# Sixteen square tiles for s, full-height products for n, and one path for all sixteen batches, in a linear attention chain

## The reference, cut to what matters

```
for i in range(12):                      # attention without a softmax, so every step is linear
    q, k, v = split(x @ Wqkv[i].T + bqkv[i])      # 16 heads of 8 channels
    att = einsum('bhqd,bhkd->bhqk', q, k) * scale
    y = einsum('bhqk,bhkd->bhqd', att, v)
    x = y @ Wproj[i].T + bproj[i] + x
x = layernorm(x0 + x)
x = layernorm(x + ffn(x))                # silu(gate) * up, hidden size 384
```

## Time and profile before

| | us |
|---|---|
| median of 3 runs | 310.84 (309.97 to 310.84) |
| span of the profiled execution | 308.2 |
| outside the span, against the median | 2.6 |
| PE busy | 302.1 (98%) |
| DVE, ACT, POOL busy | 216.9, 192.0, 133.8 |
| one layer, from an H stage to the next (L1097 at 101.95 and 121.95) | 20.00 |

### The profile page before, as it was taken

How to read it: one execution, slowest core, us unless ns; L and a number is a source line. 1 busy time by engine, 2 the same in 40 slices (tenths; PEclk the granted TensorE clock), 3 DMA queues, 4 the chain that set the end, 5 groups by cost and what they waited for, 6 DMA issues and landing times.

```text
span 308.2 us, 9599 instructions
## 1 busy us (share of the span) xinstructions
PE 302.1 (98%) x4010; PEld 283.8 (92%) x4010; DVE 216.9 (70%) x651; ACT 192.0 (62%) x459; POOL 133.8 (43%) x142
## 2 busy tenths in 40 slices
PE   8999999999999999999999999999999999999994
PEld 8989999899998998989989999899998889999983
DVE  0477586676876768758677587676765997888874
ACT  3458667686585675865758668577586276444451
POOL 3064180480723806418045072360634663655533
PEclk9999999999999999999999999999999999999999
DMA  7603003030030210300203002020000000121112
GB/s 265 265 2 113 6 6 109 4 113 2 2 115 3 74 43 4 113 4 10 105 5 113 2 3 79 4 75 6 5 0 2 2 2 0 37 64 41 34 35 72
DMA packets 8908, 14.96 MB, mean 49 GB/s; under 512 B 800, under 2 KB 5280, under 8 KB 8864
## 3 DMA queue, kind: packets, MB, share of 16 engines
q1 hardware_dynamic: 8144, 13.34, 13.1%
q10 hardware_dynamic: 720, 0.99, 0.9%
HBM read 12.23 MB, written 2.10 MB: 46 GB/s over the span
## 4 chain that ended last, share of the span: by engine, by line
PE 96%; DMA 1%; DVE 1%; POOLq 0%; issue 0%; POOL 0%; ACT 0%; SPq 0%
PE ps L988 14%; PE ps L1097 14%; PE ps L1063 13%; PE ps L1218 7%; PE ps L946 6%; PE ps L945 6%; PE ps L944 6%; PE ps L1027 4%; PE ps L1007 4%; PE ps L1206 4%; PE ps L1207 4%; PE ps L1178 2%; PE ps L1038 2%; PE ps L961 2%; PE ps L1014 2%; PE ps L999 2%
## 5 line engine op out<-in xcount | busy, mean ns | idle before, releaser
L428 POOL TENSOR_TENSOR wq_lo<-w,wq_hi 128x512 fp32r<-128x512 f32 x12 | 15.3, 1279 | 112.7 <-ACT wq_hi L551 112.7
L466 POOL TENSOR_TENSOR step_lo<-step,step_hi 128x512 fp32r<-128x512 f32 (+1 forms) x44 | 48.9, 1144 | 13.4 <-ACT step_hi L574 13.4
L944 PE MATMUL ps<-state_hi,step_hi 128*128 128x258 f32 x154 | 44.4, 288 | 0.0
L946 PE MATMUL ps<-state_hi,step_lo 128*128 128x258 f32 x154 | 43.6, 283 | 0.0
L945 PE MATMUL ps<-state_lo,step_hi 128*128 128x258 f32 x154 | 43.5, 282 | 0.0
L988 PE MATMUL ps<-w,gram 128*128 128x128 f32 x352 | 42.8, 275 | 0.0
L988 PEld LDWEIGHTS ps<-w,gram 128*128 128x128 f32 x352 | 41.9, 192 | 0.6
L547 ACT COPY gk<-ps 128x512 f32<-128x512 f32 x48 | 28.1, 586 | 21.3 <-PE ps L988 21.3
L1097 PE MATMUL ps<-step,gram 128*128 128x128 f32 x320 | 40.6, 281 | 0.0
L574 ACT CAST step_hi<-step 128x512 fp32r<-128x512 f32 (+1 forms) x44 | 24.7, 566 | 24.7 <-DVE step L764 24.7
L1097 PEld LDWEIGHTS ps<-step,gram 128*128 128x128 f32 x320 | 37.3, 192 | 1.3
(11 more groups left out here) (148 smaller groups left out, 671.2 us busy)
## 6 DMA issues: line engine op xcount, KB each, us to landing
w<-weights SPq DMA_DIRECT2D x12, 592.5 KB, 3.8
xchan<-x_chan SPq DMA_DIRECT2D x8, 256.0 KB, 4.0
out<-xchan SPq DMA_DIRECT2D x7, 256.0 KB, 2.3
xt<-x_tok SPq DMA_DIRECT2D x4, 258.0 KB, 5.5
xt<-x_tok ACTq DMA_DIRECT2D x3, 258.0 KB, 5.3
fw_int<-ffn_weights SPq DMA_DIRECT2D x1, 576.0 KB, 5.0
cst<-consts SPq DMA_DIRECT2D x1, 147.5 KB, 6.9
xt<-x_tok SPq DMA_DIRECT2D x1, 129.0 KB, 2.6
```

What stands on the lines that cost most here:

```text
L466: nc.gpsimd.tensor_tensor(step_part(step_lo, g, True), step_part(step, g, True), step_part(step_hi_f, g, True), ALU.subtract).then_inc(ste ...
L944: nc.tensor.matmul(dst, l_hi, r_hi, start=True, stop=False)
L946: return nc.tensor.matmul(dst, l_lo, r_hi, start=False, stop=True)
```

## The change

1. **S on square tiles.** A product now takes 32 rows and 32 columns: one batch, one quad. There are 64 in place of 16, in rounds of four with all four row strips and all four column strips. In round k strip i of the rows goes to strip (i + k) mod 4 of the PSUM partitions, in bank k, so that after four rounds all sixteen tiles of the array have been used once. Bank k then holds the quads of a pair of batches turned by k strips: all 128 rows of it are the s of one pair. The first half of S waits once for two blocks of `mt` (before: for one, and after its first four products for the second).
2. **N over 128 rows.** `lay_out` stores in place of the four repeated quads four copies of wq, the kth with its rows turned by k quads, so a pair's s is multiplied in one product of 128 rows that sums the four quads. Three float32 products and one of three passes for batches 0 to 7, four of three passes for batches 8 to 15: 18 products in place of 72.
3. **Waits by pair of banks.** ACT copies `s_rows` in two pieces of 256 columns, and N's first products wait for a piece each; `n_done` counts four times a layer and DVE adds the identity per group of four batches. `step`'s groups are now four neighbouring batches, and H runs group by group.
4. **No batches apart.** `b_whole`, `state_whole`, the stage at L1038 and the products at L1121 are gone. Batches 14 and 15 go through the three passes of U, and their splits, copies and low parts are made as for all the others. `mu_ready` of the last pair now comes after the copy of B's high part.

The diff, cut:

```diff
-                nc.scalar.copy(s_rows[:, 0:2, :], s_banks(0)[:, 0:2, :]).then_inc(s_low_half_ready, 1)
+                for i in range(2):
+                    nc.scalar.copy(s_rows[:, i, :], s_banks(0)[:, i, :]).then_inc(s_low_half_ready, 1)
                 act.wait_ge(s_done, at(2, 2))
...
+                for i in range(0, QUADS, 2):
+                    nc.scalar.copy(s_hi[:, i:i + 2, :], s_banks(1)[:, i:i + 2, :]).then_inc(s_hi_ready, 1)
...
-                    if g % 2 == 0:
-                        dve.wait_ge(n_done, at(2, g // 2 + 1))
+                    dve.wait_ge(n_done, at(GROUPS, g + 1))
...
-                if not first:
-                    for b in range(WHOLE):
-                        dve.wait_ge(b_whole_done, at(WHOLE, b + 1) - WHOLE)
-                        nc.vector.tensor_copy(b_whole[:, b, :], b_whole_out(b)).then_inc(b_whole_ready, 1)
...
-                    if e < SPLIT_PAIRS:
-                        dve.wait_ge(b_hi_ready, at(SPLIT_PAIRS, e + 1))
-                    else:
-                        dve.wait_ge(gram_ready, at(PAIRS, PAIRS))
                     place = 2 * (e % 2)
...
+                    dve.wait_ge(b_hi_ready, at(PAIRS, e + 1))
...
 # S
-                        pe.wait_ge(m_ready, at(GROUPS, GROUPS if h else j + 1))
-                        for i in range(QUADS):
-                            r = slice(QUAD * i, QUAD * (i + 1))
-                            place = GB * (2 * h + j)
-                            last = nc.tensor.matmul(s_banks(h)[:, i, P * j:P * (j + 1)],
-                                                    mt[r, place:place + QUADS, :].rearrange("p b i -> p (b i)"),
...
+                    pe.wait_ge(m_ready, at(GROUPS, GROUPS if h else 2))
                     for j in range(2):
+                        for k in range(QUADS):
+                            b = 2 * (QUADS * h + k) + j
+                            for i in range(QUADS):
+                                own, r = slice(QUAD * i, QUAD * (i + 1)), QUAD * ((i + k) % QUADS)
+                                last = nc.tensor.matmul(ps[r:r + QUAD, HALF_BANKS[h].start + k, P * j:P * (j + 1)], mt[own, b, :],
+                                                        wp_cent[own, :] if last_layer else w[own, s, WP:WP + P],
+                                                        start=True, stop=True)
...
 # N
+                    for k in range(QUADS):
+                        turned = slice(P * k, P * (k + 1))
+                        out_k = n_bank(h, k)
+                        if h == 0 and k < QUADS - 1:
+                            if k < 2:
+                                pe.wait_ge(s_low_half_ready, at(2, k + 1))
+                            else:
+                                pe.wait_ge(s_high_half_ready, at(1, 1))
+                            last = nc.tensor.matmul(out_k, w[:, s, WQ + P * k:WQ + P * (k + 1)], s_rows[:, k, :], start=True, stop=True)
+                        elif h == 0:
+                            pe.wait_ge(s_quad_hi_ready, at(1, 1))
+                            nc.tensor.matmul(out_k, wq_hi[:, turned], s_quad_hi[:, :], start=True, stop=False)
+                            pe.wait_ge(wq_lo_ready, at(1, 1))
+                            nc.tensor.matmul(out_k, wq_lo[:, turned], s_quad_hi[:, :], start=False, stop=False)
+                            pe.wait_ge(s_quad_lo_ready, at(1, 1))
+                            last = nc.tensor.matmul(out_k, wq_hi[:, turned], s_quad_lo[:, :], start=False, stop=True)
                         else:
+                            if k % 2 == 0:
+                                pe.wait_ge(s_lo_ready, at(2, k // 2 + 1))
+                            last = three_pass(out_k, wq_hi[:, turned], wq_lo[:, turned], s_hi[:, k, :], s_lo[:, k, :])
+                        if k % 2 == 1:
+                            last.then_inc(n_done, 1)
...
-                if not first:
-                    b_whole_stage()
...
-                        if b >= SPLIT:
-                            last = nc.tensor.matmul(ps[:, two.start + k, 0:P + 2], step[:, b, :], state_whole[:, b - SPLIT, :],
-                                                    start=True, stop=True)
-                            continue
...
-        wts[:, :, WQ + P * r:WQ + P * (r + 1)] = np.tile(wqkv[:, QUAD * r:QUAD * (r + 1)], (1, QUADS, 1))
+        wts[:, :, WQ + P * r:WQ + P * (r + 1)] = np.roll(wqkv[:, 0:P], QUAD * r, axis=1)
```

More of the change, by code:

```diff
@@ L360, in n_banks, with n_bank @@
             return ps[:, HALF_BANKS[h], 2 * P:4 * P]
+        def n_bank(h, k):
+            return ps[:, HALF_BANKS[h].start + k, 2 * P:4 * P]
         def pair_banks(e):
@@ L465, in layer @@
                     pool.wait_ge(step_hi_ready, at(GROUPS, g + 1))
-                    nc.gpsimd.tensor_tensor(step_part(step_lo, g, True), step_part(step, g, True), step_part(step_hi_f, g, True),
+                    nc.gpsimd.tensor_tensor(group(step_lo, g), group(step, g), group(step_hi_f, g),
                                             ALU.subtract).then_inc(step_lo_ready, 1)
@@ L1088, in layer @@
                     return
-                for q in range(GROUPS):
-                    if q == 2:
+                for g in range(GROUPS):
+                    if g == 2:
                         shift_stage(s, at(1, 1))
-                    pe.wait_ge(step_ready, at(GROUPS, q + 1))
-                    for g in (q // 2 * 2, q // 2 * 2 + 1):
-                        for b in range(GB * g + 2 * (q % 2), GB * g + 2 * (q % 2) + 2):
-                            last = nc.tensor.matmul(one_product(H_BANKS[g], b), gram_raw[:, b, 0:P] if first else gram[:, b, :],
-                                                    step[:, b, :], start=True, stop=True)
-                        if q % 2 == 1:
-                            last.then_inc(h_done, 1)
-                pe.wait_ge(mu_split, at(2, 2))
+                    pe.wait_ge(step_ready, at(GROUPS, g + 1))
+                    for b in range(GB * g, GB * (g + 1)):
+                        last = nc.tensor.matmul(one_product(H_BANKS[g], b), gram_raw[:, b, 0:P] if first else gram[:, b, :],
+                                                step[:, b, :], start=True, stop=True)
+                    last.then_inc(h_done, 1)
+                pe.wait_ge(mu_split, at(1, 1))
                 for e in range(PAIRS):
@@ L1133, in a_stage @@
                 for b in range(GB * g, GB * (g + 1)):
-                    left = b_whole[:, b - SPLIT, :] if b >= SPLIT else bsum[:, b, :]
-                    last = nc.tensor.matmul(one_product(A_BANKS[g], b), left, step[:, b, :], start=True, stop=True)
+                    last = nc.tensor.matmul(one_product(A_BANKS[g], b), bsum[:, b, :], step[:, b, :], start=True, stop=True)
                 last.then_inc(a_done, 1)
```

102 lines of the change are left out of this document (20 added, 82 removed).

## The result

The changed kernel takes 321.25 us (median of 4 runs, 320.8 to 322.1) against 310.46 us (309.97 to 310.84) for the kernel before on the same chip: 1.035 times the time, 95% interval 1.033 to 1.038, or 10.8 us more. The prediction was 306.5 us, and the sign is wrong. The profiled execution has a span of 319.9 us against 308.2, so 11.7 us have to be found. (The two differences are not the same, since the profiled runs are not the medians. In every run the time lies 1.8 to 1.9 us above its own span, so the profiled runs are those of 309.97 and 321.71.)

What follows compares the result with a forecast made beforehand. PE, busy 98% of the span, was taken as the bound. Middle layers at -0.40 us gave -4.0 for ten, layer 0 -0.26, the last -0.05: sum -4.3, span 303.9, time 306.5 us; eight-in-ten range 305.1 to 308.6.

Steps and rivals of the forecast that it cites:

- S's price: S: 64 square products at about 0.014 us each take 0.88 where S took 0.93 before, so nothing is lost.
- Rival 1: S: fewer than sixteen tiles run at once, so slower; 314.5 us at eight, 334 at four, about 465 singly; chance 7%.
- When S begins: Start of S: waiting for two blocks of mt moves it from 136.89 to 136.92, +0.03 us.
- ACT's copy decides N's start: Between S and N: ACT's 256-column copy ends at 138.09 and releases N at 138.15; S would allow 138.02.
- Gain 0.51 per layer: Between S and N: without B's two products, N starts at 138.15 in place of 138.66.
- N and H: N's length stays; H follows 0.12 us behind N in place of 0.23, with a usual first record: gain 0.21.
- forecast wait of 0.05 for the quad's low part: In N: the fourth quad's low part comes from POOL late, so its pass runs at 139.84 in place of 139.79.
- U: In U: two float32 products of 0.45 us together go and six passes of 0.12 come: loss 0.27 per layer.
- cover of 0.13: At U's end: the last pair's means take 1.10 us, the load is wanted at 1.23, so no cost.
- no cost: Layers: POOL gets 0.5 us more, DVE and ACT some 0.8, within their idle time, so the time does not change.
- Rows that share a bank: S: four row strips write one bank at once; allowed by the bank-and-quadrant unit, else strips go one after another.

Runs made afterwards that it cites:

- line 999 four times: The kernel before with its own square stage (16 products of kdiag times rows) issued four times in a row, result unchanged: 336.98 us.
- a quarter of the columns: The changed kernel with each of S's products on 32 of 128 columns, all instructions kept and the rest of s left out: 318.24 us.
- both streams shifted: The kernel before with part 4 of the change only, plus 24 one-column memsets on DVE and 16 one-column products on PE at the start: 319.44 us, ratio 1.028.
- part 4 alone: The kernel before without the batches apart, S and N otherwise as before: 314.56 us, ratio 1.014.

## Why the prediction was wrong, point by point

- **S's price: wrong, and this is the step that failed.** "The starts are thus spread over 0.22, about 0.014 per product ... all 64 take 0.88." The product count is paid for by the width in the first 32 records only. 64 products take 1.64, 0.0256 each. The forecast named the limit at which it would be wrong (records more than 0.011 apart); they are 0.0128 apart. I took shape, size and type as what makes a row comparable, and left out the length of the run: the row had 32 records, and it is behind the 32nd that the rate breaks. The same stage four times would have shown it before any change.
- **No term for instructions as such.** S has 256 of them in place of 64, and the sum priced only the time of the products. The stops are worth 7.2 us, as much as S's rate; the flag read that lost its cover in the last layer is 0.5 more. The page shows q8 with 36 packets in place of 33, and none of the earlier trace rows asks how fast PE uses its instructions up.
- **Rival 1 had the right place and nearly the right size of the first half.** Eight at once gave S 1.7 us and 314.5 us; measured 1.64, N 1.83 after S in place of 1.9. The time is 6.8 us above it through the stops and the end. Its reason was another one: the sixteen tiles do run together, but do not get their records fast enough. I gave it 7%, because both rows against it were of short or narrower stages.
- **When S begins: right.** S starts 1.06 after line 966 in place of 1.02; the forecast was +0.03.
- **ACT's copy decides N's start: no.** S itself does, and the copy has 0.3 to spare. "Gain 0.51 per layer" became a loss of 0.06.
- **N and H: right.** From N's start to its last group 3.07 in place of 3.06, H 0.12 behind the last pass, no long first record. The forecast wait of 0.05 for the quad's low part did not come, since N starts 0.6 later.
- **U: right.** From H to the next gk product 9.56 us, as the forecast makes it (+0.27, -0.10); no wait at the product of the means, so the cover of 0.13 held, as did "no cost" for DVE, ACT and POOL in the layers.
- **Head and end: not in the sum.** I held them for untouched. The end grew by 1.5 us, with instruction fetches beside the last transfer. The head's 0.38 goes with the later rise of PE's rate (at 5.6 us in place of 3.7), which is no work of the change that a run shows.
- **Two readings of the sum were off and changed nothing.** The time lies 1.8 above the span of its own run (309.97 against 308.2), not 2.6, so the forecast span of 303.9 makes 305.7. And ten products in 2.32 us are 0.232 each; the 0.223 is that of the six before the product of the means (1.34).
- **Rows that share a bank.** The strips ran in one bank as fast as in four banks (the changed S against line 999 four times, 1.90 both). That agrees with the unit of bank and quadrant that the Trainium skill's "PSUM — Partial Sum Buffer" gives, on bank collisions, beside the stricter rule that it quotes there. The rule of the Trainium skill's "TensorEngine Tiling (Array Packing)", Restrictions and Gotchas, Gotcha 1, that row tiles cannot use one bank at a time, did not show for these tiles, which write different quadrants of it.

No run here beats the kernel before. The only ones near or below it leave half of S out, and part 4 without the squares costs 4.3 us.

## What to carry to other kernels

Before splitting products into more and smaller tiles, count instructions: here sixteen 32x32 tiles took 128 records 12.8 ns apart, hardly closer than eight tiles (13.8), so four times the products cost nearly twice the time. A price read from a short burst is a price for that burst; take it at the length that you will run, by repeating a stage that is already there. And where an engine can use up 256 instructions in less than the 2.4 us that the next block takes, look for idle time put down to "issue" and count the instructions between its places. A changed stream length can change the run's end as well.

## What the runs showed of the hardware that was not expected

- PE stops for its instruction stream: 0.2 to 1.9 us at places a multiple of 256 instructions apart, where S runs faster than the 2.4 us from the start of a 16 KB fetch to the next record.
- With blocks fetched beside the last output transfer its last packet comes 0.4 to 1.9 us later than without.
- Sixteen tiles take records 7 to 8 ns apart for the first 32 and 12.8 apart over all 128; at 32 columns the whole stage still has 8.8 per record.
- A stop can cost more than its own length. In two runs the granted clock went to its lower level behind one (from 41.00 in the run with the stage four times, from 244.10 with a quarter of the columns). Stops of up to 1.8 us in other runs were not followed by that.
- The clock at the head. In the run with both streams shifted the 16 added products (32 records) took 6.8 us, 0.214 a record, and the gram products behind them start 0.214 apart up to 16.3 us and 0.112 apart from there (8 records between copies of ACT: 1.72, then 0.90). In part 4 alone the same 64 records were done at 12.6:

```profile
3.89 6.83 PE L919 MATMUL ps<-const-float32-0.0 128*128 128x1 f32 x32
...
10.58 10.14 PE L927 MATMUL ps<-xt 128*128 128x129 f32 x64
...
14.40 0.39 ACT L524 ACTIVATE gram_raw<-ps 128x258 f32<-128x258 f32 x1 [1.33 <-PE ps L927]
...
18.08 0.39 ACT L524 ACTIVATE gram_raw<-ps 128x258 f32<-128x258 f32 x1 [0.51 <-PE ps L927]
```

  The views print a granted clock of 1.00 for this stretch, but that is a gap: the clock records in the trace begin only at 16.31 us here (at 3.69 in the kernel before, 5.60 in the changed one, 5.47 with part 4 alone), each time with 1.0, and at that point the distance of the records falls from 0.214 to 0.112 in each of them. The half rate is thus put down to the lower level, 1.2 GHz, and what it costs is not the one column: the added records have the same 0.214 as the full products behind them. This made 8.1 us at the head, in place of the 0.5 expected; the six runs fell into two groups, near 317.3 and near 321.5. Why the clock rose 10.8 us later than in part 4 alone is not settled by one profile. What PE did before it was products of one column for 6.8 us, where the other kernels had full ones.
